# Graph-network residual kernel: the three-way split of the table done tile by tile, and the late fold groups kept in PSUM

## The reference

```python
x_src = x[src]                      # x: 6250 x 256 f32; src, dst: 100000 edges, sorted by dst
x_dst = x[dst]
theta_x = (x_dst - x_src) @ theta_w.T + theta_b
phi_x = x_src @ phi_w.T + phi_b
e = relu(theta_x + phi_x)
out = segment_max(e, dst, num_segments=6250)
out = where(isfinite(out), out, 0.0)
result = layernorm(x + out)         # over the last axis, eps 1e-5
```

## Time and profile before

| what | value |
|---|---|
| median of 3 runs | 1034.67 us |
| profiled execution, its own time | 1036.28 us |
| its span, first to last instruction | 1034.5 us |
| TensorE busy | 837.8 us (81%) |
| GpSimd busy | 771.0 us (75%) |
| VectorE busy | 693.0 us (67%) |
| ScalarE busy | 336.8 us (33%) |

### The profile page before, as it was taken

One profiled execution on the slowest core, in us unless ns is written; L12 is line 12 of the kernel. 1 busy time (PEld: TensorE's weight loads), 2 busy tenths in 40 slices (PEclk: granted clock), 3 DMA queues, 4 the chain that ended last, 5 costly groups with the idle time before them and its releaser, 6 DMA issues. The chain is left out here.

```text
span 1034.5 us, 15863 instructions
## 1 busy us (share of the span) xinstructions
PE 837.8 (81%) x3875; PEld 437.8 (42%) x3875; DVE 693.0 (67%) x1732; ACT 336.8 (33%) x701; POOL 771.0 (75%) x793
## 2 busy tenths in 40 slices
PE   5976899999999999999999999999998946650000
PEld 5832444445444544454445444454443335440000
DVE  6734666766767767676766767767765546565698
ACT  3921233333333333233333333333221121110366
POOL 6877777777777777777777777777777777775773
PEclk9988999999999999999999999999998969885555
DMA  8955667687777777767777777777866789974365
GB/s 273 368 179 179 219 221 238 220 267 228 240 243 239 248 233 240 250 221 254 236 243 241 245 240 239 231 253 233 263 221 223 231 276 311 283 239 161 117 203 177
DMA packets 116641, 243.80 MB, mean 236 GB/s; under 512 B 19632, under 2 KB 57733, under 8 KB 116549
## 3 DMA queue, kind: packets, MB, share of 16 engines
q1 hardware_dynamic: 78244, 138.69, 37.5%
q0 software_dynamic: 37728, 103.04, 34.7%
q10 hardware_dynamic: 576, 1.06, 0.3%
HBM read 127.29 MB, written 115.45 MB: 235 GB/s over the span
## 5 line engine op out<-in xcount | busy, mean ns | idle before, releaser
L465 POOL DMA_INDIRECT rows<-b_table,idx x684 | 660.6, 966 | 208.5 <-issue 176.2
L639 PE MATMUL ps_a<-work,shared 128*128 128x512 bf16 x2940 | 667.1, 382 | 37.8 <-DVE work L819 37.0
L639 PEld LDWEIGHTS ps_a<-work,shared 128*128 128x128 bf16 x2940 | 281.3, 98 | 386.2 <-DVE work L819 47.7
L549 ACT COPY hist<-acc 128x512 f32<-128x512 f32 x253 | 148.7, 588 | 489.2 <-DVE hist L863 488.9
L863 DVE SCALAR_TENSOR_TENSOR acc<-hist,reset,rows 128x256 f32<-128x256 f32 x154 | 76.1, 494 | 195.3 <-issue 157.3
L819 DVE TENSOR_SCALAR work<-batch,node 128x512 bf16<-128x512 int16 x490 | 161.5, 373 | 6.2 <-PE ps_a L639 6.2
L863 DVE SCALAR_TENSOR_TENSOR acc<-acc,reset,rows 128x256 f32<-128x256 f32 x253 | 124.7, 493 | 49.4 <-DMA rows<-b_table,idx 36.8
L863 DVE SCALAR_TENSOR_TENSOR hist<-acc,reset,rows 128x256 f32<-128x256 f32 x253 | 122.3, 484 | 27.3 <-DVE acc L863 1.8
L700 PE MATMUL ps_a<-theta_sb,shared 128*128 128x256 f32 x196 | 56.9, 446 | 36.2 <-DVE shared L909 27.5
L451 POOL DMA_INDIRECT early<-in_x,idx_first x51 | 58.7, 1150 | 17.7 <-issue 15.2
L700 PEld LDWEIGHTS ps_a<-theta_sb,shared 128*128 128x128 f32 x196 | 41.7, 223 | 51.4 <-issue 44.7
(11 more groups left out here) (129 smaller groups left out, 481.2 us busy)
## 6 DMA issues: line engine op xcount, KB each, us to landing
runmax<-hist SPq DMA_DIRECT2D x260, 384.0 KB, 3.1
direct<-b_table SPq DMA_DIRECT2D x896, 1.0 KB
rows<-b_table,idx POOLq DMA_INDIRECT x684, 3.5
b_table<-rows SPq DMA_DIRECT2D x7, 896.0 KB, 7.4
shared<-in_xt SPq DMA_DIRECT2D x49, 128.0 KB, 4.4
early<-in_x SPq DMA_DIRECT2D x12, 512.0 KB
out<-hist SPq DMA_DIRECT2D x11, 512.0 KB, 3.3
hist<-in_xt SPq DMA_DIRECT2D x7, 512.0 KB, 7.9
```

What stands on the lines that cost most here:

```text
L465: pool.indirect_dma_start(out=rows[:, PLACE[k], :], out_offset=None, in_=b_table, in_offset=bass.IndirectOffsetOnAxis(ap=idx[:, k:k + 1], ...
L549: nc.scalar.copy(hist[:, slot:slot + n - 1, :], acc[:, at:at + n - 1, :]).then_inc(s_copied, 1)
L639: mm = pe.matmul(ps_a[banks(b)[k]][:].rearrange("p j d -> p (j d)"), split[:, part, t, k * P:(k + 1) * P], hot[:, i % HOT, :], start=(t == ...
```

## The change

The two VectorE instructions of each unit of the split become 4 or 3 instructions of one tile each (256 elements on a partition), and the semaphores `s_rest` and `s_split3` count tiles instead of units. Groups 253 to 258 fold through `acc` in PSUM as the groups before them do, and ScalarE copies them; only groups 259 and 260 still write `hist` directly (`COPIED`). The looks are divided: the two results of a group that lie in `acc` are looked at one behind the other ahead of the group's third fold, into late_max in SBUF; the results that lie in `hist` are looked at into a second maximum, `late_acc`, 256 columns of PSUM. At the end one more instruction merges `late_acc` into `fix`.

```diff
+    COPIED = NG - 2
...
+        late_acc = ps_d[:, 0, :]
...
-                if g < LATE:
+                if g < COPIED:
                     sp.wait_ge(s_copied, g + 1)
...
-            pool.wait_ge(s_rest, UNITS)
+            pool.wait_ge(s_rest, NT)
...
-                if g == LATE:
+                if g == COPIED:
                     break
...
             def third_part(u):
                 tiles, _ = unit(u)
-                n = tiles.stop - tiles.start
                 dve.wait_ge(s_split2, u + 1)
-                nc.vector.scalar_tensor_tensor(split[:, 2, tiles, :], split[:, 1, tiles, :], -1.0, rest[:, u % 2, 0:n, :],
-                                               ALU.mult, ALU.add).then_inc(s_split3, 1)
+                for t in range(tiles.start, tiles.stop):
+                    nc.vector.scalar_tensor_tensor(split[:, 2, t, :], split[:, 1, t, :], -1.0,
+                                                   rest[:, u % 2, t - tiles.start, :], ALU.mult,
+                                                   ALU.add).then_inc(s_split3, 1)
...
-                nc.vector.scalar_tensor_tensor(rest[:, u % 2, 0:tiles.stop - tiles.start, :], split[:, 0, tiles, :], -1.0,
-                                               rows[:, places, :], ALU.mult, ALU.add).then_inc(s_rest, 1)
+                for t in range(tiles.start, tiles.stop):
+                    i = t - tiles.start
+                    nc.vector.scalar_tensor_tensor(rest[:, u % 2, i, :], split[:, 0, t, :], -1.0,
+                                                   rows[:, places.start + i, :], ALU.mult, ALU.add).then_inc(s_rest, 1)
...
-            def look_at(k, row):
+            looked = [0]
+
+            def look_at(k, row, best, first):
                 i = k - KEPT
                 dve.wait_ge(s_fold, k + 1)
-                if i:
-                    dve.wait_ge(s_late, i)
-                nc.vector.scalar_tensor_tensor(late_max[:], row, is_fix[:, i:i + 1], late_max[:], ALU.min,
+                if looked[0]:
+                    dve.wait_ge(s_late, looked[0])
+                looked[0] += 1
+                nc.vector.scalar_tensor_tensor(best, row, is_fix[:, i:i + 1], late_max[:] if first else best, ALU.min,
                                                ALU.max).then_inc(s_late, 1)
...
-                    new = acc[:, at + s, :] if s < n - 1 and g < LATE else hist[:, slot + s, :]
-                    if s == (n - 1 if g < LATE else 0) and g >= HELD:
+                    new = acc[:, at + s, :] if s < n - 1 and g < COPIED else hist[:, slot + s, :]
+                    if s == (n - 1 if g < COPIED else 0) and g >= HELD:
...
-                    if k > KEPT:
-                        look_at(k - 1, hist[:, before, :])
+                    if KEPT < k <= ALONE and s == 0:
+                        look_at(k - 1, hist[:, before, :], late_acc, k - 1 == KEPT + GROUP - 1)
+                    elif LATE <= g < COPIED and s == n - 2:
+                        for i in range(n - 1):
+                            look_at(START[g] + i, acc[:, at + i, :], late_max[:], False)
+                    elif k > ALONE:
+                        look_at(k - 1, hist[:, before, :], late_acc, k - 1 == KEPT + GROUP - 1)
...
-            look_at(STEPS - 1, former)
+            look_at(STEPS - 1, former, late_acc, False)
...
             dve.wait_ge(s_fixin, 16)
+            nc.vector.scalar_tensor_tensor(fix[:], late_acc, 1.0, fix[:], ALU.mult, ALU.max).then_inc(s_best, 1)
+            dve.wait_ge(s_best, 1)
             nc.vector.tensor_tensor(late_max[:], late_max[:], fix[:], ALU.max).then_inc(s_best, 1)
-            dve.wait_ge(s_best, 1)
+            dve.wait_ge(s_best, 2)
```

More of the change, by code:

```diff
@@ L505, in second_part @@
                 n = tiles.stop - tiles.start
-                act.wait_ge(s_rest, u + 1)
+                act.wait_ge(s_rest, tiles.stop)
                 nc.scalar.copy(split[:, 1, tiles, :], rest[:, u % 2, 0:n, :]).then_inc(s_split2, 1)
@@ L513, in _ @@
                     act.wait_ge(s_bout[c % 2], 16 * (c // 2))
-                    act.wait_ge(s_rest, u - 3)
+                    act.wait_ge(s_rest, unit(u - 4)[0].stop)
                 for t in range(tiles.start, tiles.stop):
@@ L630, in select @@
                     pe.wait_ge(s_split2, UNITS)
-                    pe.wait_ge(s_split3, UNITS)
+                    pe.wait_ge(s_split3, NT)
                 pe.wait_ge(s_hot, i + 1)
@@ L798, in _ @@
                 if u >= 2:
-                    dve.wait_ge(s_split3, u - 1)
-                nc.vector.scalar_tensor_tensor(rest[:, u % 2, 0:tiles.stop - tiles.start, :], split[:, 0, tiles, :], -1.0,
-                                               rows[:, places, :], ALU.mult, ALU.add).then_inc(s_rest, 1)
+                    dve.wait_ge(s_split3, unit(u - 2)[0].stop)
+                for t in range(tiles.start, tiles.stop):
+                    i = t - tiles.start
+                    nc.vector.scalar_tensor_tensor(rest[:, u % 2, i, :], split[:, 0, t, :], -1.0,
+                                                   rows[:, places.start + i, :], ALU.mult, ALU.add).then_inc(s_rest, 1)
                 if u:
@@ L817, in mark_sources @@
                 elif i == 0:
-                    dve.wait_ge(s_split3, UNITS)
+                    dve.wait_ge(s_split3, NT)
                 nc.vector.tensor_scalar(hot[:, i % HOT, :], short_sources[:, b % 2, :], node[:, t:t + 1], None,
@@ L848, in _ @@
                     dve.wait_ge(s_far, 2 * PRODUCT_OF[START[g]][0] + 2)
-                if 2 <= g < LATE:
+                if 2 <= g < COPIED:
                     dve.wait_ge(s_copied, g - 1)
```

## The result

The changed kernel takes 1026.5 us (median of 4 runs, 1024.86 to 1027.65), the kernel before 1034.46 (4 runs): 0.9924 of it, interval 0.9906 to 0.9942, a gain of 8.0 us where 6.9 were forecast. The profiled execution took 1027.65 us with a span of 1025.8, against 1036.28 and 1034.5.

The account below looks back on a forecast made before the run. GpSimd's chain of 735 gathers was taken as the bound; 5.4 (split) + 1.6 (late groups) - 0.15 (tail) = 6.9 us gained, from the median 1034.67 to 1027.8 us, range 1024.5 to 1032.0.

Parts of the forecast that it names:

- The bound: Whole span: GpSimd's 735 indirect DMAs form one chain, each some 0.947 us with 0.303 us between two.
- What holds a gather: At a gather's start: it waits for the rest of a running VectorE instruction with two SBUF inputs.
- The split's term: Split of the table: gathers lose 4.5 us in place of 9.9, a gain of 5.4 us.
- The pitch: Split: one-tile VectorE instructions of 0.42 us start 0.34 us apart; 0.40 was the upper bound.
- the factor of 1.12: Split: correction because the working gave 8.8 us of loss before the change where 9.9 were measured.
- rival D: Split: gathers fall into step, lose 2 us there and nothing late; 1024.5 us; chance 0.08, or close to it.
- The late term: Late groups: fewer instructions with two SBUF inputs cut the loss from 2.4 to 0.8 us, a gain of 1.6.
- The tail: Behind the last fold: looks through PSUM and the added merge lose 0.15 us, between nothing and 0.5.
- The cover: First table gathers: 10 us of cover left, so 1.7 us later for the table costs nothing; without it up to 3.
- A: Split: held gathers wait for a run of small instructions to end; 1041.2 us; chance 0.05 in full, 0.16 in part.
- B: Table's gathers: DMA delays the table to 78 us, only the late gain counts; 1033.2 us; 0.07 including little of either gain.
- C: Late groups: VectorE bounds them, the 1.6 us are lost; 1029.4 us; counted within the forecast's 0.64.

Follow-up runs that it names:

- the two added instructions: Changed kernel plus 7 unused VectorE instructions of 1024 elements in the split: two-input ones 1028.07 us (0.9947), one-input reductions 1023.97 us (0.9913).
- the run with one maximum: Changed kernel with looks at results in hist going into late_max in SBUF again, without the added merge: 1026.15 us, 0.993 of before.
- half a tile: Changed kernel with each split instruction cut again, to 128 elements (196 of them): 1026.07 us, 0.9923 of before.

## Why the prediction was right

**The bound** was read rightly: GpSimd's gathers are the chain, it still waits for nothing, and what a gather loses the kernel loses. The pieces of the table above add up to the span. That 8.0 us came so near to 6.9 is in part luck: in the profile the split gave 2.5 us more than forecast, the late part 0.6 more and the last row's landing 0.5, and the preparation, the middle and the end took back 1.8.

**What holds a gather** was read rightly from seven rows, and shown by the two added instructions, 4.25 us lost with two SBUF inputs and 1.71 with one, and by the folds of the middle. It was not the whole: the one-hot instructions, which read a single tensor, hold gathers too.

**The split's term** was mis-sized: 4.5 us of loss were forecast where 1.93 came (1.75, 2.08 and 1.65 in three other profiles), a gain of 7.9 in the split in place of 5.4. The pitch (0.34) and VectorE's added work were right. Two steps were wrong. The hold was put at the whole pitch of 0.34 us; in the ten profiles that have them no gather lost more than 0.26 under an instruction of 256 elements in the split, and none of the 48 that started up to 0.03 us behind one lost anything. With 0.26, and without the factor of 1.12, the same working gives 0.83 x 0.26 x 0.26 / (2 x 0.34) = 0.08 us a gather or 2.6 us for 32, an estimate. The rest is the step "a gather that comes at any time loses half a hold": the gathers are in step with the boundaries. Of the 172 that started under such an instruction 72 did so 0.20 us behind its start and lost 0.08 to 0.10, and 44 within 0.01 us of it and lost nothing. The mean was 0.06 us, not 0.16. Half of rival D, the gathers in step, was true here. 1.08 us of the gain were lost again ahead of the split, by the phase, and the first table gather came at 71.84, against some 73 forecast.

**The late term** was forecast at 1.6; the losses of the 19 gathers fell by 2.2 us in the profile. Its reasoning, a count of the instructions with two SBUF inputs, fails in the run with one maximum, where 11 more of them cost nothing: what counts is whether a gather starts under one. In the time, the part is not told from nothing (0.9997 for it alone).

**The tail** was forecast to lose 0.15 us and loses nothing (2.97 and 2.96 us): the merge fits wholly into the wait for TensorE.

**The cover** held. The wait of SyncE for the written table ended at 64.5 us, 1.6 later than before (1.7 were reckoned for the added traffic), and 7.3 us ahead of the first table gather; the first fold moved from 83.83 to 77.09:

```profile
L392 SPq EVENT_SEMAPHORE  x1: 3769/3769/3769, 60.7 to 60.7; - x1
```
```profile
77.09 0.49 DVE L871 SCALAR_TENSOR_TENSOR acc<-fix,reset,rows 128x256 f32<-128x256 f32 x1 [4.11 <-DMA rows<-b_table,idx]
```

**The rivals.** A (small instructions don't let the gather in) is no fiction: it did not come with one tile, but it is what five gathers met with half a tile, and it is the 2.07 us of the last gather. B and C did not come: between the late groups VectorE waited again for rows. The rule of the Trainium skill on many small tiles (VectorE: DVE Perf Modes, the section on the TRN2 errata) was paid by VectorE and not by the kernel: the 98 instructions took 0.42 us each where 28 had taken 1.09, beside the gathers.

## What to carry to other kernels

Where GpSimd's indirect DMAs are the chain, look for VectorE instructions that read two tensors from SBUF beside them: such a one delays the gather that starts under it until it ends. Cut them to some 256 elements, or move one operand to PSUM, which held hardly a gather here; VectorE's added overhead costs nothing while it is off the chain. Look at the one-tensor instructions too: the one-hot ones cost the changed kernel more than all its folds (7.4 and 4.1 us in the middle). Check first that GpSimd waits for nothing, on the chip that matters, since the same change gave nothing where another chain set the time.

## What was not expected of the hardware

A held gather does not always get in at the next boundary: a run of VectorE instructions of 128 elements 0.2 us apart (14 in 2.90 us) held one for 2.2 us, while most gathers under the same density lost nothing. The last gather of the kernels with the old late groups took 2.07 us in two kernels.

A reduction of 1024 elements with one SBUF input (1.22 us) holds no gather where a two-input instruction of 1.24 us holds it. That is not so of every reduction: in all fourteen profiles a gather started under the one of the preparation work (L758 of the changed kernel, 782 elements, 0.96 us), and each was held until 0.73 or 0.74 us behind its start, for up to 0.20 us. Why is open.

The 665 gathers between, in code that was never changed, lost 8.83 to 13.43 us in ten profiles of the first chips; their spread is as large as most of the effects looked for, and one profile does not give a part worth 2 us.
